# First attention of a decoder layer: query product, rotary, statistics and a remainder in another order and on other engines

## What is computed

```python
xq = (x @ Wq).reshape(b, s, 32, 16)      # 32 heads of 16
xk = (x @ Wk).reshape(b, s, 8, 16)       # 8 key/value heads
xv = (x @ Wv).reshape(b, s, 8, 16)
xq, xk = apply_rotary_emb(xq), apply_rotary_emb(xk)
scores = where(causal, einsum('bqhd,bkhd->bhqk', xq, repeat(xk)) / 4, -inf)
out = einsum('bhqk,bkhd->bqhd', softmax(scores), repeat(xv)).reshape(b, s, 512)
x = _layernorm(x + out @ Wo)
```

## Time and profile before

| | |
|---|---|
| runs shown | 807.27, 807.41, 809.64 us; median 807.41 |
| profiled execution | 806.26 us, of which the span from the first to the last instruction is 803.0 |
| TensorE busy | 755.2 us (94%), weight loads 646.9 |
| VectorE busy | 596.4 us (74%) |
| GpSimd busy | 400.6 us (50%) |
| ScalarE busy | 322.0 us (40%) |
| granted TensorE clock, mean | 0.994 |
| first attention | about 10 to 193 us of the span |

### The profile page before, as it was taken

How to read it: one execution, slowest core, us unless ns; L and a number is a source line. 1 busy time by engine, 2 the same in 40 slices (tenths; PEclk the granted TensorE clock), 3 DMA queues, 4 the chain that set the end, 5 groups by cost and what they waited for, 6 DMA issues and landing times.

```text
span 803.0 us, 13860 instructions
## 1 busy us (share of the span) xinstructions
PE 755.2 (94%) x4800; PEld 646.9 (81%) x4800; DVE 596.4 (74%) x1143; ACT 322.0 (40%) x684; POOL 400.6 (50%) x381
## 2 busy tenths in 40 slices
PE   4689999979999999999999999999999999999996
PEld 3677777769878887888888888888888888888875
DVE  4778888887877676777667667766776777688777
ACT  3545555563333333242333333233333323234335
POOL 7566666674544464444446445444544534445303
PEclk9899999999999999999999999999999999999999
DMA  9700004012263222422322342232233222141002
GB/s 232 156 18 18 16 16 121 3 26 84 54 158 80 53 55 64 103 69 52 78 52 52 73 107 55 52 78 52 55 77 103 52 53 79 27 101 31 1 1 104
DMA packets 107873, 53.52 MB, mean 67 GB/s; under 512 B 80448, under 2 KB 96960, under 8 KB 107840
## 3 DMA queue, kind: packets, MB, share of 16 engines
q1 hardware_dynamic: 107008, 51.51, 25.9%
q10 hardware_dynamic: 576, 1.05, 0.4%
q0 software_dynamic: 256, 0.52, 0.2%
HBM read 32.62 MB, written 2.10 MB: 43 GB/s over the span
## 4 chain that ended last, share of the span: by engine, by line
PE 67%; DVE 16%; issue 5%; POOL 5%; DMA 2%; ACT 2%; SPq 2%; DVEq 0%; POOLq 0%; ACTq 0%
PE bank L730 18%; PE bank L665 16%; PE bank L491 10%; DVE arena_r L1588 5%; PE s_bank L744 4%; PE bank L541 3%; PE s_bank L746 2%; PE bank L565 2%; PE bank L714 2%; DVE small L1676 2%; PE bank L885 2%; DVE arena_f L1670 1%; PE s_bank L714 1%; DMA arena_f<-in_L_attn_Wo 1%; PE s_bank L565 1%
## 5 line engine op out<-in xcount | busy, mean ns | idle before, releaser
L994 ACT ACTIVATE arena_r<-bank 128x256 fp32r<-128x256 f32 (+2 forms) x249 | 105.1, 459 | 215.7 <-PE bank L697 83.8
L730 PE MATMUL bank<-arena_r 128*128 128x512 f32 x768 | 191.4, 398 | 0.0
L665 PE MATMUL bank<-arena_r 128*128 128x512 f32 x720 | 185.2, 400 | 2.1 <-POOL arena_r L1431 1.6
L730 PEld LDWEIGHTS bank<-arena_r 128*128 128x128 f32 x768 | 139.6, 188 | 26.9
L665 PEld LDWEIGHTS bank<-arena_r 128*128 128x128 f32 x720 | 130.6, 188 | 31.4 <-POOL arena_r L1431 2.0
L491 PE MATMUL bank<-arena_r 128*128 128x256 f32 (+1 forms) x1056 | 146.7, 294 | 2.2 <-DVE arena_r L1588 1.4
L491 PEld LDWEIGHTS bank<-arena_r 128*128 128x128 f32 x1056 | 137.3, 191 | 9.4 <-DVE arena_r L1588 2.0
L1588 DVE TENSOR_TENSOR arena_r<-bank,arena_r 128x256 fp32r<-128x256 f32 (+2 forms) x217 | 99.7, 485 | 56.9 <-ACT arena_r L994 56.6
L994 ACT ACTIVATE arena_r<-arena_f 128x512 fp32r<-128x512 f32 (+2 forms) x178 | 104.5, 637 | 61.9 <-DMA arena_f<-arena_f 46.7
L1588 DVE TENSOR_TENSOR arena_r<-arena_f,arena_r 128x512 fp32r<-128x512 f32 (+1 forms) x95 | 87.2, 926 | 19.7 <-ACT arena_r L994 19.7
L1422 POOL TENSOR_TENSOR arena_f<-arena_f 128x512 f32<-128x512 f32 x30 | 39.1, 1304 | 114.5 <-DVE arena_f L1757 114.4
(11 more groups left out here) (164 smaller groups left out, 1175.8 us busy)
## 6 DMA issues: line engine op xcount, KB each, us to landing
arena_f<-arena_f SPq DMA_DIRECT2D x120, 128.0 KB, 2.5
arena_f<-in_L_xattn_Wo SPq DMA_DIRECT2D x8, 1024.0 KB, 5.9
arena_f<-in_L_xattn_Wq SPq DMA_DIRECT2D x14, 512.0 KB, 4.2
arena_f<-in_x SPq DMA_DIRECT2D x8, 256.0 KB, 2.9
arena_f<-in_x SPq DMA_DIRECT2D x1, 2048.0 KB, 17.9
arena_f<-in_L_xattn_Wk SPq DMA_DIRECT2D x8, 256.0 KB, 3.0
arena_f<-in_L_xattn_Wv SPq DMA_DIRECT2D x8, 256.0 KB, 3.3
arena_f<-in_ctx SPq DMA_DIRECT2D x8, 256.0 KB, 3.5
```

The costliest lines, as they stand in the source:

```text
L665: mm = pe.matmul(BQ2[f][:], w2q_s[a][:, e, j, f, :], xT[b][:, e, tok], start=(e == 0 and n == 0), stop=(e == EC - 1 and n == 2))
L730: mm = pe.matmul(BO2[i][:], at2[a][:, h, i * P:(i + 1) * P], w2o_s[b][:, h, :], start=(h == 0 and n == 0), stop=(h == HG - 1 and n == 2))
L994: act.activation(dst, src, ACT.Copy).then_inc(done, 1)
```

## The change

It acts on `tile_steps` of all four engines:

- TensorE: the query product of tile i + 1 is made in call i, after the second scores and ahead of the x1 transposes and the output product. The x1 transposes move from before the second scores to behind that query product. In `qk_stage` the order of groups is q, q, q, k, q, k instead of q, q, k, q, q, k; the third group waits for a first count of `s_kl`, the fourth for a second. The first scores wait for the fourth copy. The key/value product waits for the reciprocal of `total(v, 2)` (`s_rc`) instead of the last masked copy (`s_cp`).
- VectorE: `rope_q` comes ahead of `total(v, 2)`. `q_low` covers heads 0 to 15 only. `stats1`, `moments1`, `norm1` leave `tile_steps`; they stay for tiles 6 and 7, behind the loop. `x1_low` comes after the fourth maximum instead of ahead of it.
- GpSimd: the remainder of heads 16 to 31 of the queries, ahead of the key remainder; the small operations of the layer norm of tile w: `mean1` ahead of `sub(i, 0)`, `moments1` (three operations) between `sub(i, 0)` and `sub(i, 1)`.
- ScalarE: sum, sum of squares and normalisation of tile w as activations; the copy of the normalised tile into `res` and the high copy of x1 move from before `expo(i, 2)` to behind it.

```diff
@@ TensorE
-                for j, (kind, n) in enumerate((("q", 0), ("q", 1), ("k", 0), ("q", 2), ("q", 3), ("k", 1))):
+                for j, (kind, n) in enumerate((("q", 0), ("q", 1), ("q", 2), ("k", 0), ("q", 3), ("k", 1))):
                     if j == 2:
-                        pe.wait_ge(s_kl, t + 1)
+                        pe.wait_ge(s_kl, 2 * t + 1)
+                    if j == 3:
+                        pe.wait_ge(s_kl, 2 * t + 2)
...
-                pe.wait_ge(s_qke, 6 * t + 3 + 3 * (even // 2))
+                pe.wait_ge(s_qke, 6 * t + 4 + 2 * (even // 2))
...
-                b_stage(i, start)
+                if start:
+                    b_stage(i, start)
...
-                    pe.wait_ge(s_cp, 4 * i)
+                    pe.wait_ge(s_rc, 4 * i - 1)
                 kv_stage(i, start)
...
-                if oldest:
-                    x1_stage(w, i)
...
                 s_stage(i, (2, 3), start)
+                if following:
+                    b_stage(i + 1, False)
+                if oldest:
+                    x1_stage(w, i)
                 if old:
                     wo_stage(v, i, not oldest)
@@ ScalarE
+            def tile_sum1(w):
+                act.wait_ge(s_res, w + 1)
+                act.sem_inc(s_gate, 1)
+                act.activation(x1n, residual(w), ACT.Identity, accum_out=sum1).then_inc(s_ln, 1)
+
+            def tile_squares1(w):
+                act.wait_ge(s_ln, 4 * w + 2)
...
+                act.activation(x1n, residual(w), ACT.Square, bias=nmean1, scale=1.0,
+                               accum_out=var1).then_inc(s_ln, 1)
+
+            def norm1(w):
+                act.wait_ge(s_x1c, 2 * w + 1)
...
+                act.activation(x1n, residual(w), ACT.Identity, bias=shift1, scale=rstd).then_inc(s_x1n, 1)
...
+                if oldest:
+                    tile_sum1(w)
+                    tile_squares1(w)
                 if old:
                     at_high(v, not oldest)
                 expo(i, 0)
+                if oldest:
+                    norm1(w)
...
-                if oldest:
-                    act.wait_ge(s_x1n, w + 1)
-                    copy(res[:, bass.ds(w, 1), :].rearrange("p t n -> p (t n)"), x1n, s_x1c)
-                    x1_high(w)
...
                 expo(i, 2)
+                if oldest:
+                    copy(residual(w), x1n, s_x1c)
+                    x1_high(w)
                 expo(i, 3)
@@ GpSimd
+            def mean1(w):
+                pool.wait_ge(s_ln, 4 * w + 1)
...
+                pool.tensor_scalar(nmean1, sum1, -1.0 / E, None, ALU.mult).then_inc(s_ln, 1)
+
+            def moments1(w):
+                pool.wait_ge(s_ln, 4 * w + 3)
...
+                pool.tensor_scalar(var1, var1, 1.0 / E, EPS, ALU.mult, ALU.add).then_inc(s_ln, 1)
+                pool.wait_ge(s_ln, 4 * w + 4)
+                pool.tensor_tensor(rstd, var1, half, ALU.pow).then_inc(s_lp, 1)
+                pool.wait_ge(s_lp, w + 1)
+                pool.tensor_tensor(shift1, nmean1, rstd, ALU.mult).then_inc(s_x1c, 1)
...
+                pool.wait_ge(s_qh, i + 1)
+                sq = stack_q.rearrange("p h (a b d) -> p h a b d", a=2, b=2)[:, H1 // 2:]
+                pool.tensor_tensor(sq[:, :, 1], bcast(t1q.rearrange("p (h d) -> p h d", h=H1)[:, H1 // 2:], 2, 2),
+                                   f32(sq[:, :, 0]), ALU.subtract).then_inc(s_kl, 1)
                 pool.wait_ge(s_kh, i + 1)
...
                 if oldest:
-                    root1(w)
+                    mean1(w)
                 sub(i, 0, not old)
+                if oldest:
+                    moments1(w)
                 sub(i, 1, not old)
@@ VectorE
+                rope_q(i, not old)
                 if old:
                     total(v, 2)
-                rope_q(i, not old)
-                if old:
                     total(v, 3)
...
-                if oldest:
-                    stats1(w)
                 if following:
                     x_low(i + 1)
-                if oldest:
-                    moments1(w)
                 masked_max(i, 0, not old)
-                if oldest:
-                    norm1(w)
...
-                if oldest:
-                    x1_low(w)
...
                 masked_max(i, 3, not old)
+                if oldest:
+                    x1_low(w)
```

More of the change, by code:

```diff
@@ L175, in decoder_layer @@
         cid = small[0:NC, 241:242]
+        sum1, nmean1, var1, shift1 = (small[:, 152 + n:153 + n] for n in range(4))
         tot8, nmean = small[:, 224:232], small[:, 232:240]
@@ L827, in _ @@
             pe.wait_ge(c_xl, 2)
+            pe.wait_ge(s_x1l, T - 2)
             kv_proj(0, 0)
@@ L1061, in tile_steps @@
                     act.wait_ge(s_s, 4 * i)
-                for j, kind in enumerate("qqkqqk"):
+                for j, kind in enumerate("qqqkqk"):
                     act.wait_ge(s_qk, 6 * i + j + 1)
@@ L1628, in q_low @@
                 dve.wait_ge(s_qh, t + 1)
-                sq = stack_q.rearrange("p h (a b d) -> p h a b d", a=2, b=2)
-                low(sq[:, :, 1], bcast(t1q.rearrange("p (h d) -> p h d", h=H1), 2, 2), sq[:, :, 0], s_ql)
+                sq = stack_q.rearrange("p h (a b d) -> p h a b d", a=2, b=2)[:, 0:H1 // 2]
+                low(sq[:, :, 1], bcast(t1q.rearrange("p (h d) -> p h d", h=H1)[:, 0:H1 // 2], 2, 2), sq[:, :, 0], s_ql)
             def at_low(v):
@@ L1644, in stats1 @@
                 dve.wait_ge(s_res, w + 1)
+                dve.wait_ge(s_x1c, 2 * T - 5)
                 hold()
@@ L1919, in _ @@
             p_low(v, 1)
[L1920 removed]
+            dve.wait_ge(s_kl, 2 * T)
             dve.wait_ge(s_vl, T)
```

16 lines of the change are left out of this document (11 added, 5 removed).

## The result

The changed kernel takes 822.41 us (median of 4 runs, 820.35 to 823.91), the kernel before 807.34 beside it: a ratio of 1.0179, with an interval of 1.0155 to 1.0204. It is slower by 15.1 us. The forecast was 819.3 with a range of 812 to 827 and 0.90 on slower. The profiled execution took 821.4 us, of which 819.3 are the span; before 806.26 and 803.0.

What follows compares the result with a forecast made beforehand. A loop of waits through VectorE and TensorE, 20.32 us a tile, GpSimd close behind. Added 8.0 (four intervals at 2.0), 0.5, 1.8, 1.5 and 0.1 sum to 11.9 on 807.41: 819.3 us, range 812 to 827.

Steps and rivals of the forecast that it cites:

- case A: Loop: the GpSimd chain as walked lengthens each tile by 2.0 us; 815 to 824 us by itself, chance 0.70.
- Step 3: ScalarE's x1 copies stand behind the third exponential, so VectorE's x1 remainder starts at 6.8 instead of 5.87, idle 0.9.
- Step 4: VectorE's rotary products of the queries follow at 7.4, 7.36 before; the query product ended at 3.9, gain unused.
- Step 5: Third total's reciprocal done at 9.6, 7.4 before; GpSimd's third normalisation and query sum wait, key sum ends at 13.4.
- Step 6: ScalarE's query copy starts at 12.0; GpSimd's two remainders take 1.6 and 1.27; keys ready at 16.25, against 14.04.
- Step 7: TensorE's key group, now fourth, starts at 16.3; first scores at 18.1, value product ends at 22.3, period 22.3.
- Step 2: GpSimd's small layer-norm operations between the first two subtractions: about 1.5 us, covered by an existing wait, costing nothing.
- The query half: GpSimd's half of the query remainder, 512 columns: taken as 1.6 us, 1.27 at least and 2.02 at most.
- The sum: Added time: loop 8.0, into tile 2 0.5, into tile 7 1.8, tiles 0 and 1 1.5, hand-over 0.1; 11.9 us.
- B: Rival: ScalarE's x1 copy is in time, rotary starts at 6.5, period 21.4, total about 814; chance 0.12.
- C: Rival: GpSimd slower than walked, both remainders at 2.0 us, total 828; chance 0.08.
- D: Rival: faster, keys ready by 14.1, VectorE's freed 0.57 us shorten the loop, 19.75 a tile, total 804; chance 0.07.

Runs made afterwards that it cites:

- e7: Changed kernel with third total ahead of rotary, x1 copies ahead of third exponential, key group third and query remainder whole on VectorE again; 807.23 us, ratio 1.0005.
- e10: Kernel before with TensorE's new order, two waits for it, and VectorE's x1 remainder behind the fourth maximum; 804.79 us, ratio 0.9983.
- e1: Changed kernel with the third total ahead of the rotary products again on VectorE; 819.49 us, ratio 1.0137.
- e9: Changed kernel with third total ahead of rotary, x1 copies ahead of third exponential and key group third again; 813.31 us, ratio 1.0074.
- e11: Kernel before with half of the query remainder left out after tile 0, a bound and no version; 804.18 us, ratio 0.9964.
- e4: Changed kernel with transposes and their copies in the order q, q, k, q, q, k again; 820.44 us, ratio 1.0165.
- e2: Changed kernel with ScalarE's two x1 copies ahead of the third exponential again; 818.70 us, ratio 1.0140.
- e8: Kernel before with TensorE's order of the change alone; 812.16 us, ratio 1.0059.
- e12: As e9, but GpSimd does its key remainder ahead of its query half, TensorE's waits to match; 810.70 us, ratio 1.0031.

## Why the prediction was right, and where it was off

**Direction and mechanism.** Slower, by the walk of case A: each sign that it listed is in the profile. Third normalisation: 2.55 us of waiting for about 2.5 said. TensorE waits 1.64 us for VectorE at the key/value product and, at the fourth group, 0.30 us for GpSimd. VectorE waits 0.81 us ahead of the x1 remainder for 0.9, and is busy 16.5 us a tile.

**Step by step.** Step 3, x1 remainder 6.87 for 6.8. Step 4, rotary 7.48 for 7.4, with the query product unused since 3.98 (3.9 said). Step 5, reciprocal 9.64 for 9.6, key sum to 13.43 for 13.4. Step 6, query copy 12.13 for 12.0, keys ready 16.34 for 16.25. Step 7 was short: first scores at 18.38 for 18.1, period 22.52 for 22.3.

**Step 2** was too dear and right in its outcome. The product took 0.19 us and the power 0.57, where I took 0.71 for each from the earlier trace rows, which show two-column forms; the first normalisation still waits 0.17. e7 and e10 show the layer norm to be nearly free.

**The query half.** I took 1.6 and it took 1.74. Tile by tile VectorE's half starts 0.17 us ahead, both read SBUF with all their inputs, and GpSimd's ends 0.47 late on its bare 1.27. The 1.7 that the rule of "SBUF — State Buffer", section "Who interferes with whom", in the Trainium skill gave fits better than mine, and e1 and e9 show the side of that rule that I had not weighed: who starts first has the shared pair of ports for the whole instruction, and VectorE's 0.68 becomes 1.81.

**The sum.** The loop gave 8.80 for 8.0, tile 2 0.69 for 0.5, tile 7 1.83 for 1.8. The start gave 3.44 for 1.5, and the hand-over 1.10 for 0.1. The two sizes that failed are these. At the start the sum had no term for the clock: about 1.6 us lie ahead of the query product of tile 1, where e11 loses them too. The third total behind rotary was worth 1.8 us there (e1, which undoes that alone, takes 29.33 us from the first transposes to the first value product, the changed kernel 31.17), but in both profiles with the query product slowed by the clock; what it is worth at 1.00 is open. At the hand-over "the granted clock should stay" failed: it was 0.61 from 188 to 192 us. In e4 it was 1.00 there, and the stretch from the value product of tile 6 to the second attention is 25.12 us, about as before (25.00), for the changed kernel's 26.10. The other profiles agree: from the value product of tile 6 to that of tile 7 it is 17.4 to 17.6 us in the seven kernels whose profile has no fall there, the kernel before among them, and 18.3 to 18.7 in the seven that have one.

**Rivals.** B's price was right (e2), but its condition, a copy in time, did not hold. C's remainders of 2.0 did not occur. D's premise, that VectorE's 0.57 would shorten the loop if GpSimd allowed it, is what e11 measures: 0.43 a tile. D's point of 5.4 us for the six GpSimd steps is not reached: they take 6.61.

**What the working left out.** It priced TensorE's new order at nothing (its sum unchanged, the x1 transposes later) and the x1 remainder behind the fourth maximum at nothing (the same stretch). Both are right only of the pair, and that the two cancel was luck, for the working did not see it. By itself TensorE's order costs 0.8 us a tile (e8), and the remainder's new place pays that back (e10).

## What to carry to other kernels

Walk one period of a loop with every in-order queue before moving work off the fullest engine: here VectorE gave up 1.5 us a tile and the period grew by 2.2, since what it waits for and who waits for it moved too. Parts of such a change hide behind one another, so that undoing each alone explains 1.3 of 2.2 us; take them off cumulatively, and find pairs that are neutral only together. Half of an elementwise operation given to GpSimd, with all inputs in SBUF on both engines, ran one behind the other and not side by side, and ended later than the whole on VectorE; order the two so that they don't meet, and even then count GpSimd's 1.27 us against VectorE's 0.68.

## What the runs showed of the hardware

- Two remainders with SBUF inputs on VectorE and GpSimd: bare 0.68 and 1.27 us (e12). With VectorE 0.17 us ahead they took 0.76 and 1.74; with GpSimd 0.02 us ahead, 1.81 and 1.28, and the next GpSimd remainder 1.74.
- The key sum on GpSimd took 1.49 us in tile 1 of the kernel before, beside VectorE's remainder, and 0.46 in tile 1 of the changed kernel, where it ran ahead of that remainder.
- One-column operations on GpSimd: 0.19 us for a multiplication, 0.57 for a power.
- The granted clock fell to its lower level after stretches in which TensorE was idle for 1.36 and 1.54 us at a time, in some profiles and not in others with nearly the same order of work. A query product took 5.49 us at it for 3.03. In the changed kernel's loop the clock stayed at 1.00 with 3.8 us of idle time in a period of 22.5; in e8's it fell once, at 125.6 us.
